# Last rows of a graph network kernel: 42 of 98 tiles added to the output by accumulating transfers instead of being loaded, added and stored

## The chip, the cores and the metric

The kernel runs on one core of one Trainium2 chip. The metric is the device time of one execution in microseconds. Three runs of the kernel before gave 2598.17 us as their median (2597.89 to 2601.66).

## The reference, cut to what matters

The layer normalizes x (12500 rows of 256), adds to x a graph convolution (`h @ W2.T + b2` over edges) and a hyperbolic attention block, and then applies a feed-forward block to the half of the rows with the largest routing weight:

```python
x = x + gnn(xn, ...) + mix(xn, ...)          # "x2"
x = x + ffn(layernorm(x))                    # all rows get layernorm(x) added, and
                                             # only the selected ones the product below
# in ffn, with xl = layernorm(x):
weights = xl @ wr + br                       # 12500 numbers
_, idx = top_k(weights, 6250); sel = idx[:6249]
h = gelu(xl[sel] @ w1 + b1); y = h @ w2 + b2
processed = zeros.at[sel].set(y * weights[sel][:, None])
return processed + xl
```

Which rows are selected is known only after all 12500 weights are. So the kernel writes `x2 + layernorm(x2)` for every row to the output first (the "base"), computes y for every row, and at the end adds `mask * y`, where `mask` is the weight of a selected row and 0 for another.

## The kernel before, in words

The rows are cut into 98 tiles of 128 (the last has 84 rows), and the tiles into 49 pairs (`NS`). After a first stage that normalizes x, a loop of 49 steps runs edges, attention, graph convolution and, for an earlier pair, the feed-forward block (`ffn_hidden`, `ffn_project`, `ffn_result`). SyncE stores the base of each pair to `out` (L712 to L715, counted by `base_stored`). The 42 pairs 0 to 41 get their y in the loop; the seven pairs of `LATE`, 42 to 48, get it behind the loop.

y isn't kept in a buffer of its own. `ffn_result(m)` (L947) adds the bias to the PSUM bank with y of pair m and writes it over `h0T` (the SBUF tensor `resident`), at `[:, t % 2, (t // 2) * 256 ...]` for tile t, and raises `y_read`. There is one bank for y, so TensorE starts `ffn_project(m, 0)` only when `y_read` has counted m results (L1268).

While TensorE works on the late pairs, VectorE searches the threshold of the top k in `route_vector`: eleven turns, each with a small matmul (L1333), then ranks and `mask_w` (L1460), one column for each tile. `ffn_result` of the pairs 42 to 45 stands among these turns. Behind them comes `last_vector`, and beside it `last_sync` on SyncE:

- The base is read back from `out` in 14 chunks of 7 tiles (896 KB). There are eight homes for them (`flat`, in buffers that have become free). The first eight are loaded as soon as all of the base is stored (L1496), long before the mask is there. Chunks 8 to 13 are loaded again into homes whose chunk has been stored (L1500 to L1503): SyncE waits for the store of chunk c - 2 and then issues the load of chunk c + 6.
- VectorE goes through the chunks in order: for each tile one `scalar_tensor_tensor`, base + mask * y (L1522), written into the home; `row_ready` tells SyncE, which stores the chunk (L1490 to L1492).
- `ffn_result` of the pairs 46, 47 and 48 stands ahead of chunks 3, 7 and 11.
- At its end SyncE waits until all chunks are stored.

GpSimd's queue ends with `route_pool` (constants and two selects for the search); it has nothing to do in this last part. DMAs issued by SyncE go through queue q1 (hardware_dynamic), those of GpSimd through q0 (software_dynamic). The order of the work is the order in which each engine's program is written; there is no planner.

Of the kernel before, what the change touches and what calls it, by code (L numbers as in the profile page):

```python
# [6 lines left out]
ALU = mybir.AluOpType  # L7
# [6 lines left out]
P = 128  # L14
D = 256
# [34 lines left out]
def build(nc, a, out):  # L50
    x, dst, edges = a["x"], a["dst"], a["edges"]
    N, E = x.shape[0], a["n_edges"]
    NT = -(-N // P)
    NS = NT // 2
    LAST = N - (NT - 1) * P
# [9 lines left out]
    with ExitStack() as ctx:  # L65
# [6 lines left out]
        def sem(name):  # L72
            return ctx.enter_context(nc.semaphore(name))
# [10 lines left out]
        h0T = resident[:, :].rearrange("p (c n) -> p c n", c=C)  # L84
# [30 lines left out]
        def view(base, at, *shape):  # L115
            n = 1
            for s in shape:
                n *= s
            v = base[:, at:at + n]
            if len(shape) == 2:  # L120
                v = v.rearrange("p (a b) -> p a b", b=shape[1])
            if len(shape) == 3:
                v = v.rearrange("p (a b c) -> p a b c", b=shape[1], c=shape[2])
            return v
# [41 lines left out]
        def tables_rows(pool):  # L166
            pool.dma_start(rows[:, :, :].bitcast(I32), dst.rearrange("(c p j) -> p c j", p=P, j=P)
                           ).then_inc(rows_landed, 16)

        def tables_load(pool):  # L170
            pool.wait_ge(ends_out, 2)
            for k in range(2):
                pool.dma_start(tile_ends_dram[k], endsT[:EC, k, :]).then_inc(ends_stored, 16)
            pool.wait_ge(ends_stored, 32)
            pool.dma_start(ends_bc[:NT], tile_ends_dram.rearrange("k c j -> k (c j)").partition_broadcast(NT)
                           ).then_inc(ends_landed, 16)
# [41 lines left out]
        def tables_pool(pool):  # L218
            g = nc.gpsimd
            g.iota(iota[:, :], [[1, P]], base=0, channel_multiplier=0,  # L220
                   allow_small_or_imprecise_dtypes=True).then_inc(consts_ready, 1)
            g.iota(iota_m, [[1, EC * P]], base=0, channel_multiplier=0,
                   allow_small_or_imprecise_dtypes=True).then_inc(consts_ready, 1)
            g.iota(thr, [[0, 1]], base=0, channel_multiplier=P,
                   allow_small_or_imprecise_dtypes=True).then_inc(consts_ready, 1)
            g.memset(zeros, 0.0).then_inc(consts_ready, 1)
            g.memset(ones, 1.0).then_inc(consts_ready, 1)
            pool.wait_ge(consts_ready, 5)
            g.affine_select(out=ident[:, :], in_=zeros, compare_op=ALU.not_equal, fill=1.0, base=0,
                            pattern=[[-1, P]], channel_multiplier=1).then_inc(consts_ready, 1)  # L230
            g.memset(mixW, 0.0).then_inc(consts_ready, 1)
# [426 lines left out]
        base_stored = sem("base_stored")  # L658
        x3_turned, x3T_ready, hid_done, hid_read = sem("x3_turned"), sem("x3T_ready"), sem("hid_done"), sem("hid_read")
        y_done, y_read = sem("y_done"), sem("y_read")  # L660
# [14 lines left out]
        LATE = list(range(m_next, NS))  # L675
# [268 lines left out]
        def y_rows(m):  # L944
            return h0T[:, :, 2 * m * P:2 * (m + 1) * P]

        def ffn_result(m):  # L947
            nc.vector.wait_ge(y_done, m + 1)
            nc.vector.tensor_tensor(y_rows(m), Y_BANK[:, :].rearrange("p (t d) -> p t d", d=D),
                                    fb2_row[:, :].unsqueeze(1).broadcast_to([P, 2, D]), ALU.add).then_inc(y_read, 1)  # L950
# [418 lines left out]
        ROUND_TRIES = [1, 1] + [TRIES] * ROUNDS  # L1369
        VISITS = 4  # L1370
        at = lambda n, w: work[:, n:n + w]
        wm, vv, flag, gt, eq, pre, incl, selm = (at(100 * q, NT) for q in range(8))
        mask_w = at(800, NT)
# [14 lines left out]
        def only_nodes(pool, dst_ap, src_ap):  # L1388

            return nc.gpsimd.affine_select(out=dst_ap, in_=src_ap, compare_op=ALU.is_ge, fill=LOWEST, base=N - 1,  # L1390
                                           pattern=[[-P, NT]], channel_multiplier=-1)

        def route_pool(pool):
            pool.wait_ge(slot_used, RING + NT * SLOTS)
            nc.gpsimd.memset(all_ones, 1.0).then_inc(route_consts, 1)
            pool.wait_ge(route_consts, 1)
            nc.gpsimd.affine_select(out=below, in_=all_ones, compare_op=ALU.is_gt, fill=0.0, base=0,
                                    pattern=[[1, P]], channel_multiplier=-1).then_inc(route_consts, 1)
            for b, value in enumerate(steps):
                ins = nc.gpsimd.memset(bits[:, b:b + 1], value)  # L1400
            ins.then_inc(route_consts, 1)
            pool.wait_ge(out_ready, 2 * NS)
            only_nodes(pool, wm, route_w[:, :]).then_inc(wm_ready, 1)
            pool.wait_ge(v_scaled, 1)
            only_nodes(pool, vv, vv).then_inc(vv_ready, 1)
# [57 lines left out]
        CH = 7  # L1463
        NCH = NT // CH
        flat = [view(rings, D * (2 + CH * n), CH, D) for n in range(3)]
        flat += [view(work, 2560 + CH * D * n, CH, D) for n in range(3)]
        flat += [view(weights, CH * D * n, CH, D) for n in range(2)]
        HOMES = len(flat)
        assert NT % CH == 0 and HOMES < NCH <= 2 * HOMES - 2
        row_landed = [sem(f"row_landed{c}") for c in range(NCH)]  # L1470
        row_stored = [sem(f"row_stored{c}") for c in range(NCH)]
        row_ready = sem("row_ready")

        def home(c):
            return flat[c % HOMES]

        def last_sync(sp):
            def parts(c):
                if c < NCH - 1:
                    return [(out[c * CH * P:(c + 1) * CH * P].rearrange("(t p) d -> p t d", p=P), home(c))]  # L1480
                first = c * CH * P
                return [(out[first:first + (CH - 1) * P].rearrange("(t p) d -> p t d", p=P), home(c)[:, 0:CH - 1]),
                        (out[first + (CH - 1) * P:N], home(c)[:LAST, CH - 1])]

            def load(c):
                for rows_, buf in parts(c):
                    sp.dma_start(buf, rows_).then_inc(row_landed[c], 16)

            def store(c):
                sp.wait_ge(row_ready, c + 1)  # L1490
                for rows_, buf in parts(c):
                    sp.dma_start(rows_, buf).then_inc(row_stored[c], 16)  # L1492

            sp.wait_ge(base_stored, 16 * NS + 16)
            sp.wait_ge(w2_done, NS)
            for c in range(HOMES):  # L1496
                load(c)
            for c in range(NCH):
                store(c)
                again = c - 2 + HOMES  # L1500
                if HOMES <= again < NCH:
                    sp.wait_ge(row_stored[c - 2], 16)
                    load(again)  # L1503
            for c in range(NCH):
                sp.wait_ge(row_stored[c], 32 if c == NCH - 1 else 16)

        def last_vector(dve):
            v = nc.vector
            seen = 1 + (len(ROUND_TRIES) + 1) // VISITS
            result_at = {}  # L1510
            for n, m in enumerate(LATE[seen:]):
                result_at[3 + 4 * n] = m
            assert LATE[0] * 2 >= (max(result_at) + 1) * CH
            for c in range(NCH):
                if c in result_at:
                    ffn_result(result_at[c])
                if c * CH + CH > LATE[0] * 2:
                    dve.wait_ge(y_read, NS)
                dve.wait_ge(row_landed[c], 32 if c == NCH - 1 else 16)
                for n in range(CH):  # L1520
                    t = c * CH + n
                    ins = v.scalar_tensor_tensor(home(c)[:, n], h0T[:, t % 2, (t // 2) * 2 * P:(t // 2 + 1) * 2 * P],  # L1522
                                                 mask_w[:, t:t + 1], home(c)[:, n], ALU.mult, ALU.add)
                ins.then_inc(row_ready, 1)

        @block.sync
        def _(sp):
            norm_sync(sp)
            main_sync(sp)
            last_sync(sp)  # L1530

        @block.gpsimd
        def _(pool):
            tables_rows(pool)
            tables_pool(pool)
            tables_load(pool)
            params_pool(pool)
            tables_bounds(pool)
            main_pool(pool)
            route_pool(pool)  # L1540

        @block.scalar
        def _(act):
# [4 lines left out]
        @block.vector  # L1548
        def _(dve):
            tables_vector(dve)  # L1550
            norm_vector(dve)
            main_vector(dve)
            route_vector(dve)
            last_vector(dve)
# [56 lines left out]
```

## Time and profile before

| | us |
|---|---|
| median of three runs (lowest, highest) | 2598.17 (2597.89, 2601.66) |
| the profiled execution, its own time | 2600.18 |
| its span (first to last instruction) | 2598.6 |
| mean granted TensorE clock | 0.982 of full speed |
| busy: TensorE matmul, VectorE, GpSimd, ScalarE | 2466.0, 1804.1, 1768.3, 1462.8 |
| DMA moved, mean over the span | 333.45 MB, 128 GB/s |

The table is read so: TensorE is busy 95% of the span, and all the rest of the kernel hides behind it. The profiled execution took 1.58 us more than its span, and 2.01 us more than the median of the runs. The change touches only the part from about 2542 us on, so the stretches of that part matter more than any mean.

### The profile page before, as it was taken

The numbers are of one execution on the slowest core, as the hardware profiler recorded it, in microseconds if no ns is written. First come the engines' busy times: TensorE is split into PE (matmuls) and PEld (weight loads), VectorE is DVE, ScalarE is ACT, GpSimd is POOL, SyncE is SP. The second block draws the span as 40 slices with busy tenths as digits, with TensorE's granted clock in tenths as the row PEclk, the third lists the DMA queues.
The fourth block names the chain that finished last, engine by engine and source line by source line (L and its number), as shares of the span: only waits on it lengthen the run. The fifth ranks groups of instructions, "written<-read, shape, count | busy, mean of one in ns | idle before, by whom it ended". The sixth has DMA issues, their size and how long they took to land.

```text
span 2598.6 us, 42298 instructions
## 1 busy us (share of the span) xinstructions
PE 2466.0 (95%) x12655; PEld 2168.7 (83%) x12655; DVE 1804.1 (69%) x5988; ACT 1462.8 (56%) x3513; POOL 1768.3 (68%) x1879
## 2 busy tenths in 40 slices
PE   4788999999999999999999999999999999999997
PEld 3677888888888888888888888888888888888886
DVE  6847676676776767767667676676866767767657
ACT  3756565565655656556555565565655656556431
POOL 2037777777777777777777777777777777777500
PEclk9898999999999999999999999999999999999998
DMA  7643434444344344444444434444444444343338
GB/s 231 193 133 101 128 113 121 124 117 129 116 121 125 114 121 123 121 126 115 119 124 117 130 113 121 123 116 126 117 120 124 116 125 117 114 129 114 97 117 282
DMA packets 192006, 333.45 MB, mean 128 GB/s; under 512 B 46286, under 2 KB 133964, under 8 KB 191672
## 3 DMA queue, kind: packets, MB, share of 16 engines
q0 software_dynamic: 86752, 238.17, 32.0%
q1 hardware_dynamic: 105018, 92.42, 11.1%
q8 instruction: 113, 1.85, 0.3%
q14 instruction: 123, 1.01, 0.1%
HBM read 291.99 MB, written 38.46 MB: 127 GB/s over the span
## 4 chain that ended last, share of the span: by engine, by line
PE 79%; DVE 10%; DMA 5%; ACT 5%; issue 1%; POOL 0%; SPq 0%; DVEq 0%; POOLq 0%
PE bank L1165 24%; PE qkv L1260 13%; PE bank L1272 12%; PE bank L1179 10%; PE bank L1209 6%; PE qkv L1189 4%; DMA work<-in_x 4%; PE qkv L1188 2%; PE bank L1225 2%; PE bank L1234 2%; DVE rings L968 2%; PE bank L1199 2%; DVE work L386 1%; DVE work L415 1%; ACT work L804 1%
## 5 line engine op out<-in xcount | busy, mean ns | idle before, releaser
L774 POOL DMA_INDIRECT rings<-xn_dram,window x1764 | 1742.4, 988 | 617.5 <-issue 382.3
L1165 PE MATMUL bank<-rings 128*128 128x256 f32 x3528 | 884.7, 380 | 17.4 <-DVE rings L968 14.2
L1165 PEld LDWEIGHTS bank<-rings 128*128 128x128 f32 x3528 | 656.9, 190 | 110.7 <-DVE rings L968 24.0
L968 DVE TENSOR_SCALAR rings<-iota,window_dst,window 128x128 f32<-128x128 f32 x1764 | 561.5, 363 | 142.2 <-PE bank L1165 127.9
L1260 PE MATMUL qkv<-work,ffn_weights 128*128 128x256 f32 x1568 | 364.4, 381 | 0.0
L1272 PE MATMUL bank<-ffn_weights,work 128*128 128x256 f32 x1568 | 361.9, 379 | 0.0
L864 ACT ACTIVATE work<-qkv,fb 128x256 f32<-128x256 f32 x392 | 160.1, 473 | 311.4 <-PE qkv L1260 310.9
L1272 PEld LDWEIGHTS bank<-ffn_weights,work 128*128 128x128 f32 x1568 | 297.2, 190 | 40.0
L1260 PEld LDWEIGHTS qkv<-work,ffn_weights 128*128 128x128 f32 x1568 | 295.0, 191 | 38.2
L1179 PE MATMUL bank<-resident,weights 128*128 128x256 f32 x1176 | 280.4, 382 | 0.0
L1179 PEld LDWEIGHTS bank<-resident,weights 128*128 128x128 f32 x1176 | 225.4, 192 | 31.1
L791 ACT ACTIVATE work<-qkv 128x1536 bf16<-128x1536 f32 x98 | 142.2, 1451 | 188.2 <-PE qkv L1189 188.2
L846 ACT ACTIVATE work<-bank 128x512 f32<-128x512 f32 x49 | 29.3, 598 | 315.5 <-PE bank L1217 315.5
L1189 PE MATMUL qkv<-weights,work 128*128 128x128 f32 x1176 | 205.0, 279 | 0.0
L1209 PE MATMUL bank<-weights,work 128*128 128x256 f32 x784 | 191.0, 387 | 0.1
L1188 PE MATMUL qkv<-ident,work 128*128 128x128 f32 x588 | 163.5, 278 | 23.5 <-ACT work L810 22.1
L1189 PEld LDWEIGHTS qkv<-weights,work 128*128 128x128 f32 x1176 | 182.2, 195 | 1.4
L877 ACT ACTIVATE work<-bank,cols 128x256 f32<-128x256 f32 x294 | 150.1, 566 | 57.6 <-PE bank L1179 57.6
L1026 DVE SCALAR_TENSOR_TENSOR work<-work,cols,bank 128x256 f32<-128x256 f32 x98 | 46.5, 475 | 189.3 <-PE bank L1165 189.3
L1209 PEld LDWEIGHTS bank<-weights,work 128*128 128x128 f32 x784 | 149.5, 193 | 27.1 <-ACT work L821 5.8
L1031 DVE TENSOR_TENSOR work<-work,b_row 128x512 f32<-128x512 f32 x49 | 34.1, 696 | 138.7 <-DMA work<-in_x 138.6
L1188 PEld LDWEIGHTS qkv<-ident,work 128*128 128x128 f32 x588 | 85.7, 146 | 34.5 <-issue 32.2
(243 smaller groups left out, 3346.2 us busy)
## 6 DMA issues: line engine op xcount, KB each, us to landing
rings<-xn_dram,window POOLq DMA_INDIRECT x1764, 2.8
xn_dram<-work SPq DMA_DIRECT2D x14, 896.0 KB, 7.7
work<-xn_dram SPq DMA_DIRECT2D x49, 256.0 KB
work<-in_x SPq DMA_DIRECT2D x48, 256.0 KB
out<-work SPq DMA_DIRECT2D x48, 256.0 KB
work<-in_x SPq DMA_DIRECT2D x9, 896.0 KB, 5.7
rings<-out SPq DMA_DIRECT2D x6, 896.0 KB, 8.8
out<-rings SPq DMA_DIRECT2D x6, 896.0 KB, 6.3
```

Source lines behind the costliest of these rows:

```text
L774: nc.gpsimd.indirect_dma_start(out=msg[q][:, :], out_offset=None, in_=xn_dram[:, :], in_offset=bass.IndirectOffsetOnAxis(ap=window[t % WIN ...
L791: s.activation(sq_dump, qkv.rearrange("p r i s c -> p (r i s c)"), ACT.Square, accum_out=nsq[h]).then_inc(nsq_ready, 1)
L864: ins = s.activation(hT[:, k], HID_BANK[q][:, e * D:(e + 1) * D], ACT.Gelu_apprx_tanh, bias=fb1[:, k:k + 1])
L877: ins = s.activation(h2T[:, k], H1_BANK[q][:, e * D:(e + 1) * D], ACT.Relu, scale=bn_a[:, k:k + 1], bias=bn_b[:, k:k + 1])
L968: v.tensor_scalar(sel[k % SEL_RING], iota[:, :], window_dst[b][:, k % SLOTS:k % SLOTS + 1], window[b][:, k % SLOTS, 2:3].bitcast(F32), ALU ...
L1165: te.matmul(agg[h][:, 0:D], sel[k % SEL_RING], msg[q], start=first, stop=last, skip_group_check=True).then_inc(slot_used, 1)
L1179: ins = te.matmul(H1_BANK[q][:, e * D:(e + 1) * D], wqkvT[:, c, k * P:(k + 1) * P], h0T[:, c, 2 * i * P:2 * (i + 1) * P], start=(c == 0), ...
L1188: te.transpose(qkv[:, k // 2, k % 2, 0, :], lhs, ident[:, :])
L1189: ins = te.matmul(qkv[:, k // 2, k % 2, 1, :], lhs, mixW[:, k, :], start=True, stop=True)
L1209: ins = te.matmul(FT_BANK[h][:, 0:D], outT[:, c], wresT[:, c], start=(c == 0), stop=(c == 3))
L1260: ins = te.matmul(HID_BANK[q][:, e * D:(e + 1) * D], fw1[:, c, k * P:(k + 1) * P], x3T[:, c], start=(c == 0), stop=(c == C - 1))
L1272: ins = te.matmul(Y_BANK[:, h * D:(h + 1) * D], hT[:, k, h * P:(h + 1) * P], fw2[:, k], start=(k == 0 and h == 0), stop=(k == HC - 1), ski ...
```

## The change

Only chunks 0 to 7 (tiles 0 to 55, pairs 0 to 27) are still loaded, added and stored by SyncE. For tiles 56 to 97 (pairs 28 to 48) VectorE multiplies y by the mask in place, and GpSimd issues transfers from `h0T` to `out` that add to what is in DRAM (`accum_op=ALU.add`). There are five such handovers, of 7, 7, 4, 2 and 1 pairs, with two transfers each (even tiles, odd tiles), so ten transfers. VectorE's order is written out in `ORDER` ("add" is a chunk as before, "scale" the new step for a range of pairs, "result" is `ffn_result`). `last_pool` is called at the end of GpSimd's program, behind `route_pool`.

```diff
-        row_landed = [sem(f"row_landed{c}") for c in range(NCH)]
-        row_stored = [sem(f"row_stored{c}") for c in range(NCH)]
-        row_ready = sem("row_ready")
+        ORDER = [("scale", 28, 35), ("add", 0), ("result", LATE[seen]), ("add", 1), ("scale", 35, 42), ("add", 2), ("add", 3),
+                 ("add", 4), ("result", LATE[seen + 1]), ("add", 5), ("scale", 42, 46), ("add", 6), ("add", 7), ("scale", 46, 48),
+                 ("result", LATE[seen + 2]), ("scale", 48, 49)]
+        SCALED = [o[1:] for o in ORDER if o[0] == "scale"]
+        row_landed = [sem(f"row_landed{c}") for c in range(HOMES)]
+        row_stored = sem("row_stored")
+        row_ready, y_scaled, row_added = sem("row_ready"), sem("y_scaled"), sem("row_added")
...
             for c in range(HOMES):
-                load(c)
-            for c in range(NCH):
-                store(c)
-                again = c - 2 + HOMES
-                if HOMES <= again < NCH:
-                    sp.wait_ge(row_stored[c - 2], 16)
-                    load(again)
-            for c in range(NCH):
-                sp.wait_ge(row_stored[c], 32 if c == NCH - 1 else 16)
+                sp.dma_start(home(c), rows_of(c)).then_inc(row_landed[c], 16)
+            for c in range(HOMES):
+                sp.wait_ge(row_ready, c + 1)
+                sp.dma_start(rows_of(c), home(c)).then_inc(row_stored, 16)
+            sp.wait_ge(row_stored, 16 * HOMES)
+            sp.wait_ge(row_added, 32 * len(SCALED))
+
+        def last_pool(pool):
+            pool.wait_ge(base_stored, 16 * NS + 16)
+            for u, (a_, b_) in enumerate(SCALED):
+                pool.wait_ge(y_scaled, u + 1)
+                for h in range(2):
+                    if b_ == NS and h == 1:
+                        pool.dma_start(out[(NT - 1) * P:N], h0T[:LAST, h, 2 * a_ * P:2 * b_ * P], accum_op=ALU.add
+                                       ).then_inc(row_added, 16)
+                    else:
+                        rows_ = out[2 * a_ * P:2 * a_ * P + (b_ - a_) * 2 * P - (P if b_ == NS else 0)]
...
+                            rows_ = rows_.rearrange("(m c p) d -> c p m d", c=2, p=P)[h]
+                            pool.dma_start(rows_, h0T[:, h, 2 * a_ * P:2 * b_ * P].rearrange("p (m d) -> p m d", d=D),
+                                           accum_op=ALU.add).then_inc(row_added, 16)
 
         def last_vector(dve):
...
+            for what, *which in ORDER:
+                if what == "result":
+                    ffn_result(which[0])
+                elif what == "add":
+                    c = which[0]
+                    dve.wait_ge(row_landed[c], 16)
+                    for n in range(CH):
+                        t = c * CH + n
+                        ins = v.scalar_tensor_tensor(home(c)[:, n], y_of(t), mask_w[:, t:t + 1], home(c)[:, n],
+                                                     ALU.mult, ALU.add)
+                    ins.then_inc(row_ready, 1)
+                else:
+                    a_, b_ = which
+                    dve.wait_ge(y_read, b_)
+                    for t in range(2 * a_, 2 * b_):
+                        ins = v.tensor_scalar(y_of(t), y_of(t), mask_w[:, t:t + 1], None, ALU.mult)
+                    ins.then_inc(y_scaled, 1)
...
             route_pool(pool)
+            last_pool(pool)
```

## Rows read from the trace of the kernel before

**Rows 1.** The page: busy time of each engine.

```profile
PE 2466.0 (95%) x12655; PEld 2168.7 (83%) x12655; DVE 1804.1 (69%) x5988; ACT 1462.8 (56%) x3513; POOL 1768.3 (68%) x1879
```

**Rows 2.** Stretches of the last part: busy us (instructions) by engine, clock, DMA share, GB/s.

```profile
2494.30:2516.00 21.70, 21.70 (x110) 19.02 (x110) 14.97 (x42) 6.30 (x16) 0.27 (x1) 1.00 1.01 322
2545.60:2557.00 11.40, 11.40 (x56) 10.06 (x55) 11.39 (x29) 3.60 (x9) 0.00 (x0) 1.00 0.90 272
2557.00:2575.00 18.00, 18.00 (x87) 15.86 (x86) 15.52 (x39) 4.82 (x12) 0.00 (x0) 1.00 1.08 382
2575.00:2596.00 21.00, 4.14 (x20) 3.30 (x18) 11.14 (x28) 0.00 (x0) 0.00 (x0) 0.66 1.09 385
2596.00:2598.60 2.60, 0.00 (x0) 0.00 (x0) 0.00 (x0) 0.00 (x0) 0.00 (x0) 0.50 0.23 80
```

**Rows 3.** The chain of waits from 2570 us on: start us, us, what.

```profile
2573.96 5.20 PE bank L1272 x24
2579.15 0.02 issue
2579.18 0.17 DVE resident L949
...
2585.01 3.17 DVE work L1522 x8
```

**Rows 4.** Timeline of VectorE behind the mask: start us, us, instruction, idle before.

```profile
2542.40 0.26 DVE L1460 TENSOR_TENSOR work<-work,route_w 128x98 f32<-128x98 f32 x1
2542.70 8.40 DVE L1522 SCALAR_TENSOR_TENSOR rings<-resident,work,rings 128x256 f32<-128x256 f32 x21
2551.11 0.69 DVE L949 TENSOR_TENSOR resident<-bank,fb_row 128x512 f32<-128x512 f32 x1
...
2565.36 0.69 DVE L949 TENSOR_TENSOR resident<-bank,fb_row 128x512 f32<-128x512 f32 x1 [2.48 <-PE bank L1272]
...
2579.18 0.69 DVE L949 TENSOR_TENSOR resident<-bank,fb_row 128x512 f32<-128x512 f32 x1 [2.04 <-PE bank L1272]
```

**Rows 5.** Timeline of SyncE's DMA issues in the last part: start us, us, transfers.

```profile
2545.59 5.91 SPq L1492 DMA_DIRECT2D out<-rings  x3
...
2583.61 9.72 SPq L1492 DMA_DIRECT2D out<-work  x4
```

**Rows 6.** DMA packets from 2542 us to the end: queue, packets, MB, share of 16 engines.

```profile
q1 hardware_dynamic: 18180, 18.26, 93.1%
```

**Rows 7.** Durations (ns, min/median/max) by line, first and last start us.

```profile
L267 DVE TENSOR_SCALAR resident<-resident,rings x1: 1087/1087/1087, 56.2 to 56.2; 98x1664 f32<-98x1664 f32 x1
L1452 DVE TENSOR_SCALAR work<-work x1: 273/273/273, 2537.7 to 2537.7; 128x98 f32<-128x98 f32 x1
L1522 DVE SCALAR_TENSOR_TENSOR rings<-resident,work,rings x42: 475/478/485, 2542.7 to 2576.7; 128x256 f32<-128x256 f32 x42
```

**Rows 8.** A run of seven two-column tensor_scalar in the first stage, timeline.

```profile
91.81 2.35 DVE L415 TENSOR_SCALAR work<-rings,work 128x256 f32<-128x256 f32 x7
```

**Rows 9.** Timeline of TensorE, project of pair 48 (L1272).

```profile
2570.34 1.89 PE L1272 MATMUL bank<-ffn_weights,work 128*128 128x256 f32 x8
```

**Rows 10.** GpSimd's direct DMA issues: ns min/median/max; then time to landing us.

```profile
L167 POOL DMA_DIRECT2D resident<-in_dst x1: 1357/1357/1357, 1.5 to 1.5; - x1
L193 POOL DMA_DIRECT2D weights<-in_w_pw x4: 572/573/619, 21.7 to 23.5; - x4
tile_ends_dram<-rings POOLq DMA_DIRECT2D x2, 6.5 KB, 1.7
rings<-xn_dram,window POOLq DMA_INDIRECT x1764, 2.8
```

**Rows 11.** DMA queues of the whole span: packets, MB, share of 16 engines.

```profile
q0 software_dynamic: 86752, 238.17, 32.0%
```

**Rows 12.** GpSimd's issues and VectorE's tensor_scalar side by side in the loop, durations.

```profile
L774 POOL DMA_INDIRECT rings<-xn_dram,window x1764: 942/946/1465, 163.8 to 2450.0; - x196
L968 DVE TENSOR_SCALAR rings<-iota,window_dst,window x1764: 327/343/574, 165.9 to 2456.8; 128x128 f32<-128x128 f32 x196
```

More of the change, by code:

```diff
@@ L1468, in build, with rows_of @@
         HOMES = len(flat)
-        assert NT % CH == 0 and HOMES < NCH <= 2 * HOMES - 2
-        row_landed = [sem(f"row_landed{c}") for c in range(NCH)]
-        row_stored = [sem(f"row_stored{c}") for c in range(NCH)]
-        row_ready = sem("row_ready")
+        LOADED = HOMES * CH
+        assert LOADED % 2 == 0 and LOADED < 2 * LATE[0]
+        seen = 1 + (len(ROUND_TRIES) + 1) // VISITS
+        ORDER = [("scale", 28, 35), ("add", 0), ("result", LATE[seen]), ("add", 1), ("scale", 35, 42), ("add", 2), ("add", 3),
+                 ("add", 4), ("result", LATE[seen + 1]), ("add", 5), ("scale", 42, 46), ("add", 6), ("add", 7), ("scale", 46, 48),
+                 ("result", LATE[seen + 2]), ("scale", 48, 49)]
+        SCALED = [o[1:] for o in ORDER if o[0] == "scale"]
+        assert LATE[seen + 2] == NS - 1 and SCALED[0][0] * 2 == LOADED and SCALED[-1][1] == NS
+        row_landed = [sem(f"row_landed{c}") for c in range(HOMES)]
+        row_stored = sem("row_stored")
+        row_ready, y_scaled, row_added = sem("row_ready"), sem("y_scaled"), sem("row_added")
         def home(c):
-            return flat[c % HOMES]
+            return flat[c]
+        def rows_of(c):
+            return out[c * CH * P:(c + 1) * CH * P].rearrange("(t p) d -> p t d", p=P)
         def last_sync(sp):
[L1478 to L1492, printed above, removed]
             sp.wait_ge(base_stored, 16 * NS + 16)
@@ new lines, in last_sync @@
+            sp.wait_ge(row_stored, 16 * HOMES)
[10 more added lines that the diff above has]
+                        rows_ = out[2 * a_ * P:2 * a_ * P + (b_ - a_) * 2 * P - (P if b_ == NS else 0)]
+                        if b_ == NS:
+                            pool.dma_start(rows_, h0T[:, h, 2 * a_ * P:2 * b_ * P], accum_op=ALU.add).then_inc(row_added, 16)
+                        else:
+                            rows_ = rows_.rearrange("(m c p) d -> c p m d", c=2, p=P)[h]
+                            pool.dma_start(rows_, h0T[:, h, 2 * a_ * P:2 * b_ * P].rearrange("p (m d) -> p m d", d=D),
+                                           accum_op=ALU.add).then_inc(row_added, 16)
@@ L1507, in last_vector @@
         def last_vector(dve):
             v = nc.vector
[L1509 to L1524, printed above, removed]
+            y_of = lambda t: h0T[:, t % 2, (t // 2) * 2 * P:(t // 2 + 1) * 2 * P]
@@ new lines, in last_vector @@
+            for what, *which in ORDER:
[9 more added lines that the diff above has]
+                    ins.then_inc(row_ready, 1)
+                else:
+                    a_, b_ = which
[3 more added lines that the diff above has]
+                    ins.then_inc(y_scaled, 1)
```

## The prediction
> **What bounds the kernel now.** I read the page first: TensorE is busy 95% of the span [rows 1], so over most of it nothing else counts. The change begins behind the mask, so I then read the last part by stretches. The reader is to see there where TensorE stops: it is full until 2575, has 4.14 us left in the next stretch, and nothing behind that, while the DMA engines run at a share of 1.08 to 1.09 and 382 to 385 GB/s from 2557 to 2596 [rows 2]. The chain of waits gives the place: TensorE ends at 2579.15, and the chain goes over to VectorE, whose last addition ends at 2588.18 (2585.01 + 3.17) [rows 3]. The chain stops at that last instruction; the span goes on to 2598.6. What lies between is SyncE's stores, whose last issues go from 2583.61 to 2593.33 although VectorE has long handed everything over [rows 5]. So the last part is bound by the transfers: 18.26 MB by q1 [rows 6]. That is 12.80 MB of stores (12500 rows of 1 KB) and 5.46 MB of loads of chunks 8 to 13 (5332 rows). At 385 GB/s these take 47.4 us; they have 2545.6 to 2596.6. The end of full flow, 2596.6, I get from the last stretch: 80 GB/s over 2.6 us is 0.21 MB or 0.54 us at full rate [rows 2]. Behind it stand 2.0 us of last packets and the final wait. The missing 3.6 us are the start (the first store) and the thinner stretch up to 2557, at 272 GB/s [rows 2].
>
> Two floors lie below: TensorE with 2579.15, and VectorE behind it.
>
> **VectorE, step by step.** An addition costs 8.40/21 = 0.400 us in a run, 0.396 behind the first (its duration is 0.478, it overlaps the next by 0.082) [rows 4, 7]. 42 go. 42 `tensor_scalar` with one column come. The trace has none of 256 columns; with one column operand, 98 columns take 273 ns and 1664 take 1087 [rows 7], 0.52 ns for each more, so 256 take 0.355 us. Less the same overlap that is 0.273 in a run. The bound from above is the two-column form at 2.35/7 = 0.336 [rows 8], beyond that 0.396. I take 0.273: VectorE has 42 x (0.396 - 0.273) = 5.2 us less.
>
> The schedule from 2542.70 [rows 4]:
> - scale 28-35 (14 tiles, 3.8 us) to 2546.5; add 0 to 2549.3; result 46 waits for TensorE until 2551.11, as y isn't there before (1.8 us idle, behind it add 1 and the second handover wait); free at 2551.7.
> - add 1 to 2554.5, scale 35-42 to 2558.3, add 2 to 4 to 2566.6. Result 47 is read at once (y is there since 2565.36) and counted at 2567.3. TensorE needs it at 2570.34 [rows 9]: 3.1 us of cover. If a multiplication cost 0.396, 28 of them would take 3.4 us more, and TensorE would be held by 0.4.
> - add 5 to 2570.0, scale 42-46 to 2572.2, add 6 and 7 to 2577.8, scale 46-48 to 2578.9; result 48 waits for TensorE to 2579.18, as before; scale 48 ends at 2580.4.
>
> So VectorE ends at 2580.4 instead of 2588.2, 7.8 us earlier. That is worth something only if the transfers end with it.
>
> **SyncE.** Six chunks of loads and six of stores go, with their waits. It stores eight chunks, each ready earlier than the transfers get to it, except chunk 0 (2549.4 in place of 2545.6).
>
> **GpSimd.** It has one instruction of 0.27 us in the stretch from 2494.3 and none behind it [rows 2], so its ten issues delay nothing of its own. An issue costs 0.57 us for small ones and 1.36 for the one with 1664 runs [rows 10]; one with 896 rows I put at 1.0, bounds 0.6 to 1.4. Ten are under 10 us beside 34. Of the first one the wakeup and about 1.4 us until data flow are on the path: first data at 2546.5 + 0.1 + 1.4 = 2548.0. Of the last ones nothing is, if the queue is still full then. If it is not, two issues of 0.6 and a landing of 2.8 [rows 10] end the kernel: 2580.4 + 0.1 + 1.2 + 2.8, some 2584.5 to 2585.5.
>
> **The transfers, which decide.** Plain stores: 7168 rows, 7.34 MB, 19.1 us at 385 GB/s. Accumulated rows: 5.46 MB, 14.2 us multiplied by f, where f is the price of an accumulated row in plain ones. The trace shows no accumulating transfer, so f is bounded. Below: it costs no more than the store that it replaces, f = 1, 14.2 us. Above: an accumulated row is fetched from DRAM and from SBUF and written once, thus what the load and the store of before moved, and it does that at the rate of q0's packets: 238.17 MB in 32.0% of 2598.6 us (831.6 us) are 286 GB/s [rows 11], so f = 2 x 385/286 = 2.7, 38.3 us. Nearest is f = 2: two fetches at the rate of the saturated stretch, in which loads and stores are mixed and together reach 385 [rows 2]. I take f = 2, 28.4 us. Sum: 2548.0 + 19.1 + 28.4 = 2595.5, plus 2.0 behind the flow: 2597.5. On the way the queues never run dry: handover 1 and chunk 0 keep them until 2559.9, chunk 1 until 2562.3, and handover 2 is issued at 2558.4.
>
> So 18.26 MB of packets become 7.34 stored and twice 5.46: the same 47.4 us. What was saved is the thinner stretch at the start (3.6 us before, against 2548.0 - 2545.6 = 2.4 now): 1.1 us. The profiled execution would be 2600.18 - 1.1 = 2599.1, and the median of the runs 2598.17 - 1.1 = **2597.1**.
>
> From the trace, a load and a store together flow as fast as stores alone, so the fetches seem to share one limit in each DMA engine. The Trainium skill says the same of an added reduction (Collectives: The Full Stack, "The bandwidth ceiling"): the addition itself is free, the two source reads on one ring halve the rate, 62.28 against 32.35 GB/s. By that ratio f would be 1.93, an estimate, and the end 1.0 us earlier. No row here shows it. The same section has 32.35 GB/s on two DMA engines; as an estimate 16 would add at 259 GB/s, so f = 1.49, which is the first rival at its f of 1.5.
>
> **Rivals.**
> 1. Accumulating is cheaper than load and store (f 1.0 to 1.7): the second fetch is partly hidden behind the first. For it: the copies are of 1 KB runs, and a copy may be limited at its SBUF end rather than in the engine. Against it: mixed loads and stores use both directions and still stop at 385. With f = 1.5: 2588.4 + 2.0 = 2590.4, median 2590.0. With f = 1 the queues run dry (the stores and handovers are waited for), and the last issues set 2585.5, median 2585.1.
> 2. The other side: an accumulated row flows no faster than q0's packets. Place: the 5332 rows on q0; price at 286 GB/s of fetches: 38.3 us in place of 28.4, end 2607.4, median 2607.0. It decides against the change from f = 2.43 on (158 GB/s of accumulated rows), where the end is 5.2 us behind that of before. For it: q0's share in the loop. Against it: those packets are small batches of 128 scattered rows, in which an engine waits more than it moves.
> 3. GpSimd's issues are late. In the loop GpSimd's issue takes up to 1.465 us against 0.946, and the tensor_scalar up to 0.574 against 0.343 [rows 12]: they do get in each other's way, half a us at a time. The Trainium skill has this as a lock (SBUF — State Buffer, "SBUF: two separate sides"): GpSimd can't write descriptors during a two-port operation of VectorE; the trace agrees in sign. Here handover 1 meets only additions, and ten issues by 0.5 us are 5 us on an idle engine; on the path are 1.0 us at most. It costs more only where the queue's room for rows runs out and GpSimd waits in the middle of a handover: then q0 stops between handovers, and I put 3 to 8 us on it, median 2601 to 2605.
> 4. TensorE waits for result 47 (the dear multiplication): 0.4 us, and only visible under rival 1.
>
> **How the numbers follow.** A change of under 0.2% (5.2 us) can't be told from none. The forecast (f from 1.70 to 2.43, ends 2593.3 to 2603.6) gets 0.40, all of it no change. Rival 1 gets 0.34, all faster. Rival 2 gets 0.20 and rival 3 0.06, slower in all. The forecast's own range is 2593 to 2603; the other cases reach to 2585 and 2607, beyond that where a row is dearer still. The range 2587 to 2609 leaves out the cheapest tenth and the dearest.
>
> **What would show it.** The packets of q0 in the last part: their share times the stretch, over 5.46 MB, gives f at once. DMA share near 1.09 from 2548 to about 2595 says the forecast; a share falling before 2585 says rival 1; q0 still alone at 2600 says rival 2. VectorE's last instruction should end at 2580.4, each multiplication taking 0.355, and TensorE should still end at 2579.2. Wrong would make it: any f outside 1.7 to 2.43, or a hole in the flow between 2548 and 2590.

## The result, and the profile after

The changed kernel takes 2602.61 us (median of 22 runs), the kernel before 2598.59 beside it: ratio 1.0013, 95% interval 1.0007 to 1.0019. So it is slower by 0.13%: 3.4 us by the ratio, 4.0 by the two medians. That is less than the 0.2% that the prediction called no change, but beyond the interval. The prediction had the time in its range and the sign of its small difference wrong: 1.1 us faster.

The page of the changed kernel, its span and engines [rows 1]:

```profile
span 2599.9 us, 42287 instructions
PE 2461.7 (95%) x12655; PEld 2167.7 (83%) x12655; DVE 1800.4 (69%) x5988; ACT 1460.8 (56%) x3513; POOL 1780.4 (68%) x1889
```

The span of one execution says little, as the loop ahead of the mask varies by some us. So I compare the last part, from the first instruction that uses the mask to the end of the span. It starts at 2542.70 before [rows 4] and at 2540.42 here (timeline of VectorE, columns as in [rows 4]):

```profile
2540.12 0.26 DVE L1460 TENSOR_TENSOR work<-work,route_w 128x98 f32<-128x98 f32 x1
2540.42 3.77 DVE L1533 TENSOR_SCALAR resident<-resident,work 128x256 f32<-128x256 f32 x14
2544.10 2.86 DVE L1526 SCALAR_TENSOR_TENSOR rings<-resident,work,rings 128x256 f32<-128x256 f32 x7
2548.83 0.69 DVE L949 TENSOR_TENSOR resident<-bank,fb_row 128x512 f32<-128x512 f32 x1 [1.87 <-PE bank L1272]
...
2564.19 0.69 DVE L949 TENSOR_TENSOR resident<-bank,fb_row 128x512 f32<-128x512 f32 x1
...
2577.62 0.83 DVE L1533 TENSOR_SCALAR resident<-resident,work 128x256 f32<-128x256 f32 x2
```

The last part is 2598.6 - 2542.7 = 55.9 us before and 2599.9 - 2540.4 = 59.5 us after: 3.6 us more, which agrees with the timed runs. Times below that are "behind the mask" count from there.

The stretches that answer to [rows 2], two shorter ones around the first data, and the queues between 2562 and 2590:

```profile
2545.60:2557.00 11.40, 11.40 (x54) 10.06 (x53) 9.53 (x29) 2.51 (x6) 3.46 (x3) 1.00 1.00 186
2557.00:2575.00 18.00, 18.00 (x87) 15.85 (x87) 18.00 (x49) 4.68 (x11) 5.11 (x4) 1.00 1.17 244
2575.00:2596.00 21.00, 1.85 (x9) 1.30 (x7) 2.86 (x8) 0.00 (x0) 4.24 (x4) 0.59 1.16 260
2546.50:2547.00 0.50, 0.50 (x4) 0.45 (x3) 0.46 (x2) 0.00 (x0) 0.50 (x2) 1.00 0.00 0
2547.00:2547.50 0.50, 0.50 (x4) 0.45 (x3) 0.00 (x0) 0.00 (x0) 0.50 (x1) 1.00 0.48 39
2547.25:2550.00 2.75, 2.75 (x15) 2.42 (x14) 1.17 (x3) 0.00 (x0) 1.07 (x1) 1.00 1.15 155
```

```profile
q0 software_dynamic: 3290, 3.29, 72.6%
q1 hardware_dynamic: 3408, 3.42, 44.5%
```

The reader is to see three things. From 2557 on the DMA engines are full, as they were before: share 1.16 to 1.17, against 1.08 to 1.09 (a share above 1 says that packets of one engine overlap in time). An accumulated row is counted once (5.46 MB for 42 tiles in all), so 240 GB/s here are 117 accumulated and 122 stored. The two queues send about as many packets of 1 KB there, 3290 and 3408. And the first data come at 2547.25, 6.8 us behind the mask, where the stores of before began 3.8 us behind it. GpSimd's part of that:

```profile
2544.81 3.51 POOL L1512 DMA_DIRECT2D out<-resident  x2 [51.96 <-DVE resident L1533]
...
2556.26 3.27 POOL L1512 DMA_DIRECT2D out<-resident  x2 [7.94 <-DVE resident L1533]
...
L1533 DVE TENSOR_SCALAR resident<-resident,work x42: 334/349/571, 2540.4 to 2578.1; 128x256 f32<-128x256 f32 x42
```

A handover has two issues, and the second starts before the first has ended. The two of 896 rows take 3.51 us together in handover 1 and 3.27 in handover 2, so 1.75 and 1.64 for each; the very first takes 1.82 by itself.

### The profile page after: what moved, and what is told of

The parts are those of the page before. It is cut to its first block, busy times and chain, and to the rows that moved or that the text cites. A ratio compares the mean times of both kernels' runs of the same rounds, so it can differ in the third digit from the quotient of the medians.

```text
span 2599.9 us, 42287 instructions
## 1 busy us (share of the span) xinstructions
PE 2461.7 (95%) x12655; PEld 2167.7 (83%) x12655; DVE 1800.4 (69%) x5988; ACT 1460.8 (56%) x3513; POOL 1780.4 (68%) x1889
## 3 DMA queue, kind: packets, MB, share of 16 engines
q14 instruction: 123, 1.01, 0.1%
## 4 chain that ended last, share of the span: by engine, by line
PE 79%; DVE 10%; ACT 4%; DMA 4%; issue 1%; SPq 0%; POOL 0%; POOLq 0%; DVEq 0%
PE bank L1165 25%; PE qkv L1260 13%; PE bank L1272 12%; PE bank L1179 10%; PE bank L1209 6%; PE qkv L1189 4%; DMA work<-in_x 3%; PE qkv L1188 2%; PE bank L1225 2%; PE bank L1234 2%; PE bank L1199 2%; DVE rings L968 2%; DVE work L386 1%; DVE work L415 1%; PE bank L1246 1%
## 5 line engine op out<-in xcount | busy, mean ns | idle before, releaser
L1272 PE MATMUL bank<-ffn_weights,work 128*128 128x256 f32 x1568 | 362.0, 379 | 0.0
L1272 PEld LDWEIGHTS bank<-ffn_weights,work 128*128 128x128 f32 x1568 | 297.6, 190 | 39.7
```

Of the source, the lines that this page charges most:

```text
L1272: ins = te.matmul(Y_BANK[:, h * D:(h + 1) * D], hT[:, k, h * P:(h + 1) * P], fw2[:, k], start=(k == 0 and h == 0), stop=(k == HC - 1), ski ...
```

## The experiments

Every run's last part, read as above, and its timed ratio to the kernel before where there is one. The first four experiments (e1 to e4) ran on a chip that took 2992 us for the kernel before, with a granted clock of 0.93 in place of 0.98; VectorE's schedule behind the mask was the same there to 0.1 us, so these four are read by their last part.

| run | last part, us | ratio to before (interval) |
|---|---|---|
| kernel before; again | 55.9; 55.8 | |
| changed kernel | 59.5 | 1.0013 (1.0007, 1.0019) |
| e1_plain | 47.9 | 0.9975 (0.9949, 1.0000) |
| e2_alone | 46.0 | 0.9974 (0.9947, 1.0000) |
| e3_long_runs | 55.0 | 0.9996 (0.9967, 1.0025) |
| e4_chunk_first | 59.8 | 1.0004 (0.9975, 1.0034) |
| e5_last_merged | 59.8 | 1.0017 (1.0008, 1.0026) |
| e6_stores_first | 61.2 | 1.0020 (1.0010, 1.0029) |
| e7_14_tiles | 55.9 | 1.0006 (0.9996, 1.0015) |
| e8_long_alone | 45.8 | |
| e9_stores_queued | 51.1 | |
| e11_small_first; again (e13) | 57.4; 57.0 | 0.9995 (0.9963, 1.0026); 1.0011 (1.0002, 1.0020) |
| v1_reload_by_gpsimd | 55.6 | 1.0001 (0.9992, 1.0010) |
| v2_first_in_pieces | 55.3 | 0.9996 (0.9987, 1.0005) |
| v3_ninth_home | 53.0 | 0.9995 (0.9986, 1.0004) |
| v4_five_more_tiles | 52.0 | 0.9985 (0.9958, 1.0013) |
| v5_whole_first | 52.4 | 0.9990 (0.9981, 0.9999) |

**b0_before_again.**

> The kernel before, unchanged, for a second reading of the last part from the first addition behind the mask to the end: 55.9 us in the first profile. Theory: this stretch does not depend on what the chip or the throttle does to the loop before it, so 55.9 within 0.3. Rival: it varies by some us from execution to execution; then differences under 2 us between the profiles say nothing.

55.8: the last part repeats to 0.1 us here, and to 0.4 in the one relative of the changed kernel that has two profiles (e11 and e13). The changed kernel itself has one.

**What the addition costs: e1_plain, e2_alone, e9_stores_queued.**

```diff
-  pool.dma_start(rows_, ..., accum_op=ALU.add)
+  pool.dma_start(rows_, ...)
```

> The changed kernel with its ten transfers as plain writes: the addition to DRAM is left out, so tiles 56 to 97 get only mask * y. VectorE, GpSimd's issues and SyncE are as in the changed kernel. Theory A (the transfers' own flow is the cost: an accumulated row costs 2.2 plain ones): 12.8 MB at 385 GB/s are 33 us, less than the 37 us that VectorE takes from the mask to its last handover, so the end is set by the last issues and landing: some 42 to 44 us behind the mask (59.5 in the changed kernel), time about 0.6% below the changed one. Theory B (the late start and GpSimd's issues, 1.2 to 2.4 us each, are the cost and the flow is not): the end comes at least 55 us behind the mask, time within 0.2% of the changed one. GpSimd's issue of 896 rows: 1.75 us if the addition does not make it dearer, 1.2 or less if it does.

The end moved from 59.5 to 47.9 us: theory A. It missed my 42 to 44, since the writes flowed at 322 GB/s and not at 385. GpSimd's two issues of 896 rows fell from 3.51 to 2.00 us together, from 1.75 to 1.00 for each, and the first data came 6.0 us behind the mask in place of 6.8. One more thing changed than the addition: q0's plain writes are packets of 4 KB in the trace (1326 of them), the accumulating ones of 1 KB (5332). An issue of 896 rows has 896 packets when it accumulates and 224 when it doesn't, and that may be what shortens it (see the price of a run). What larger packets alone do to the flow of plain writes wasn't tried; SyncE's plain stores are of 1 KB and flow at 341 GB/s alone (below).

```profile
2945.50:2985.00 39.50, 30.12 (x142) 26.18 (x140) 29.23 (x81) 7.20 (x17) 6.02 (x9) 0.91 0.98 322
2943.57 2.00 POOL L1512 DMA_DIRECT2D out<-resident  x2 [51.94 <-DVE resident L1532]
```

```diff
-  for c in range(HOMES):
-      sp.wait_ge(row_ready, c + 1)
-      sp.dma_start(rows_of(c), home(c)).then_inc(row_stored, 16)
+  sp.wait_ge(row_ready, HOMES)
```

> The changed kernel with SyncE's eight stores left out (tiles 0 to 55 stay without mask * y). The accumulating transfers have the DMA engines for themselves. Theory A1 (an accumulated row costs two fetches and some more, whatever is beside it): 385/2.2 = 175 GB/s while handovers 1 and 2 flow. Theory A2 (alone each row waits for its own fetch, and only a second queue fills these gaps): about 140 GB/s as in the first 3 us of the changed kernel's flow, and then 3.67 MB of handovers 1 and 2 take 26 us. Rival B: no slower than stores, 300 GB/s or more, with idle engines between handovers. End: set by the last handovers under all, 43 to 46 us behind the mask, about 0.5% below the changed kernel.

Both A1 and A2 missed, on the dear side. A stretch of e2_alone in which q0 has work throughout:

```profile
2947.40:2951.40 4.00, 4.00 (x20) 3.53 (x19) 4.00 (x14) 2.10 (x6) 0.00 (x0) 1.00 1.23 193
```

By steps of 2 us the full stretches read 188 to 200 GB/s, typically 195. Against 385 that is f = 1.97. (In e6_stores_first q0 is alone for 18 us, at 198 GB/s: 1.94.) Against the 341 GB/s of plain stores that are alone too (e9_stores_queued, next) it is 1.75. The Trainium skill's ratio for a reduction against a copy (Collectives: The Full Stack, "The bandwidth ceiling"), 1.93, agrees with the first; the like comparison, each alone, gives less.

```diff
+  v.memset(at(1900, 1), 0.0).then_inc(mask_made, 1)       # at the mask
-      sp.wait_ge(row_ready, c + 1)
+      sp.wait_ge(row_landed[c], 16)                        # behind one wait for mask_made
-  last_pool(pool)
```

> The changed kernel reduced to its eight plain stores: they are all issued as soon as the mask is there, without VectorE's additions (left out, as are the accumulating transfers). TensorE works beside them as before. It gives the rate of queued stores alone. Reading 1: 385 GB/s, as for the last stores of the kernel before; then a mixed flow of 240 GB/s (117 accumulated, 122 stored) means 5.8 us for each accumulated MB against 5.1 alone, a price of mixing of 0.7 us per MB, and the 331 to 347 GB/s of stores early in the last part are VectorE's rate of supply. Reading 2: 350 GB/s or less; then mixing costs 0.4 or less, and the stores that lose their loads lose rate.

Reading 2, as far as it goes. Queued stores alone in e9_stores_queued, and the last stores of the kernel before:

```profile
2542.00:2560.00 18.00, 11.29 (x55) 9.59 (x53) 1.50 (x6) 3.84 (x9) 0.00 (x0) 0.94 1.04 341
```

```profile
2590.00:2596.00 6.00, 0.00 (x0) 0.00 (x0) 0.00 (x0) 0.00 (x0) 0.00 (x0) 0.50 1.09 386
```

341 GB/s here, also while TensorE stood still (344 from 2554 to 2560, where the row has no matmul); yet stores behind a mixed flow run at 385. Why stores alone have two rates is not settled.

**The price of a run: e3_long_runs, e8_long_alone.**

```diff
-  rows_ = rows_.rearrange("(m c p) d -> c p m d", c=2, p=P)[h]
-  pool.dma_start(rows_, h0T[...].rearrange("p (m d) -> p m d", d=D), accum_op=ALU.add)
+  rows_ = rows_.rearrange("(c p m) d -> c p (m d)", c=2, p=P)[h]
+  pool.dma_start(rows_, h0T[...], accum_op=ALU.add)
```

> The changed kernel, but the rows of a handover are laid so that each partition adds to neighbouring rows in DRAM: one run of 7 KB (4 KB, 2 KB) in place of 7 (4, 2) of 1 KB. It adds y to the wrong rows; bytes, order and waits are the same. Theory A1 (the price is bytes: two fetches for one write): f stays at 2.0 to 2.2, time within 0.2% of the changed kernel, at best 3 us less. Theory A2 (the price is a fixed one for each run of a row): f falls to 2.0 or below, flow of both queues together from 240 to over 270 GB/s, the end 4 to 8 us earlier. GpSimd's issue: down from 1.75 us to about 0.8 if it goes by the number of runs.

> Both changes at once: runs of 7, 4 and 2 KB in DRAM (the rows added to are not the right ones) and SyncE's eight stores left out. With 1 KB runs and the engines for themselves the accumulating transfers flow at 197 GB/s. Theory bytes (two fetches for each write are all of the price): 190 to 210 GB/s here too, and the 4.5 us that long runs brought beside the stores are the mixing, which gets cheaper with long runs. Theory run (a fixed price for each run): 220 GB/s or more alone.

With long runs the end came 4.5 us earlier. Of that 0.8 is the earlier start: two issues took 1.91 us in place of 3.51 (e3_long_runs), and data came 6.0 us behind the mask. So a long issue isn't owed to the addition alone: with 128 packets an accumulating issue takes 0.96 us, with 896 it takes 1.75, and the plain one of e1_plain with 224 takes 1.00. No run has both forms with the same number of packets, so what the addition itself adds to an issue stays open. With the engines to itself (e8_long_alone) the flow was 219 GB/s (208 to 222 by 2 us):

```profile
2931.90 1.91 POOL L1512 DMA_DIRECT2D out<-resident  x2 [51.94 <-DVE resident L1533]
```

```profile
2553.20:2557.20 4.00, 4.00 (x20) 3.54 (x19) 3.63 (x9) 1.02 (x3) 0.00 (x0) 1.00 1.07 219
```

So part of the price goes by the run, as A2 had it, but most of it by bytes. With the best 2 us of each, 200 and 222 GB/s on 16 engines, a run of 1 KB takes 82 ns and one of 7 KB 517: that is 10 ns for the run and 72 for each KB, which two fetches of 36 would make. A plain 1 KB row at 385 takes 42.6 ns. The two forms differ in the rows' places in DRAM too, which I didn't separate.

**Order and start: e4_chunk_first, e6_stores_first, e11_small_first.**

```diff
-  ORDER = [("scale", 28, 35), ("add", 0), ("result", ...
+  ORDER = [("add", 0), ("scale", 28, 35), ("result", ...
```

> The changed kernel with chunk 0 ahead of the first handover on VectorE, nothing else. In the changed kernel data flow from 6.9 us behind the mask on, in the kernel before from 3.9. Theory start (the flow is continuous to the end, so each us of an earlier start is one gained): stores from 3.9 us on, while GpSimd issues the first handover at 7.2 and not at 4.4; 2.4 us of work done before, end 2 to 2.5 us earlier, time 0.1% below the changed kernel, that is level with before. Rival (the last handovers set the end): no change.

59.8: no gain. Chunk 0 flowed early, and then the engines stood idle until the later handover's data came (e4_chunk_first):

```profile
2927.00:2929.50 2.50, 2.50 (x13) 2.21 (x12) 2.36 (x9) 0.00 (x0) 0.00 (x0) 1.00 0.94 315
2929.50:2932.00 2.50, 2.50 (x13) 2.19 (x12) 0.77 (x2) 0.00 (x0) 2.01 (x2) 1.00 0.02 7
```

This run also shows that VectorE isn't what makes an issue long. The first one starts here while VectorE is idle (2929.4 to 2931.2), and it takes 1.82 us (the two 3.51), as in the changed kernel beside VectorE's additions:

```profile
2929.99 3.51 POOL L1512 DMA_DIRECT2D out<-resident  x2 [54.73 <-DVE resident L1533]
```

```diff
-  ORDER = [("scale", 28, 35), ("add", 0), ("result", LATE[seen]), ("add", 1), ...
+  ORDER = [("add", 0), ("add", 1), ("add", 2), ("result", LATE[seen]), ("add", 3), ("add", 4), ("add", 5), ("scale", 28, 35),
+           ("add", 6), ("result", LATE[seen + 1]), ("add", 7), ("scale", 35, 42), ("scale", 42, 46), ("scale", 46, 48),
```

> The changed kernel with VectorE's order turned: the chunks that SyncE stores come first (the first handover stands behind chunk 5, the second behind chunk 7), so that stores and accumulating transfers overlap little. Bytes and transfers are the same. Flow seen so far: accumulating alone 197 GB/s (5.1 us per MB), mixed with stores 240 GB/s together, from which an accumulated MB costs 5.5 to 5.8 us. Theory mixing (the two queues hinder each other, 0.5 us or so for each accumulated MB): end 56.5 to 57.5 us behind the first instruction after the mask, against 59.5. Rival (an accumulated row costs the same beside stores; order does not matter): 59 to 60. Rival gap (the first handover is later, and the engines are idle before it): over 60.

61.2: the gap won, and the profile shows it. Stores alone flow no faster than VectorE finishes chunks (0.917 MB in 2.77 us, 331 GB/s), the engines are idle for 2 us and more before the handover's data, and q0 alone is left at the end (e6_stores_first):

```profile
2564.00:2566.00 2.00, 2.00 (x11) 1.77 (x10) 2.00 (x6) 0.00 (x0) 2.00 (x2) 1.00 0.01 1
2582.00:2600.00 18.00, 0.00 (x0) 0.00 (x0) 0.00 (x0) 0.00 (x0) 3.55 (x4) 0.50 1.23 198
```

So the order is worth some us, but this run can't price the mixing.

```diff
-  ORDER = [("scale", 28, 35), ("add", 0), ...
+  ORDER = [("scale", 28, 29), ("scale", 29, 35), ("add", 0), ...
```

> The changed kernel with its first handover cut in two, pair 28 alone and then pairs 29 to 34. The first data should flow from about 3.6 us behind the mask and not from 6.9. Unlike chunk 0 first, this leaves no hole, as GpSimd goes on issuing. Theory start (the late first data are part of the loss and are kept to the end): end 1.5 to 3 us earlier, 56.5 to 58 us against 59.5 behind the mask. Rival (supply in the first ten us bounds the flow, as with the first chunk in pieces, where an earlier start brought 0.3): under 0.5 us.

> The changed kernel with pair 28 handed over alone ahead of pairs 29 to 34, timed in more rounds than the first time, where the interval was too wide (0.9963 to 1.0026) for a difference of 2 us. From the profile (57.4 us behind the mask against 59.5 in the changed kernel and 55.8 before): time 0.06% above the kernel before, against 0.13% for the changed kernel. If the late first handover were not part of the loss, 0.13% again.

57.4 and 57.0: 2.1 to 2.5 us of the 3.6 come back, so the late start is the larger part of the loss. The data start 3.9 us earlier, but not all of that is kept, as they flow thinly at first. The timed rounds (1.0002 to 1.0020) are consistent with that and don't prove it. First data in e11_small_first flow 3 us behind the mask (2552.83):

```profile
2555.00:2556.00 1.00, 1.00 (x8) 0.90 (x7) 1.00 (x5) 0.38 (x2) 1.00 (x2) 1.00 0.31 22
2557.00:2560.00 3.00, 3.00 (x16) 2.64 (x15) 2.50 (x7) 0.00 (x0) 2.92 (x2) 1.00 0.66 69
```

**How many tiles, and the last handover: e7_14_tiles, e5_last_merged.**

```diff
 (in the kernel before)
-  for c in range(NCH): store(c) ...
+  for c in range(NCH - 2): store(c) ...
+  if c == 3: scale(42, 46)      # behind result 46
+  if c == 8: scale(46, 48)
+  scale(48, 49)                 # behind the last chunk; six accumulating transfers
```

> The kernel before with only its last two chunks (tiles 84 to 97, pairs 42 to 48) accumulated by GpSimd, in handovers of 4, 2 and 1 pairs; chunks 8 to 11 are reloaded and stored by SyncE as before. Theory rate (each accumulated tile costs 0.2 to 0.3 plain ones more than load and store): a third of the 42 tiles, a third of the 3.6 us: 57.1 us behind the mask. Theory start (the 3.6 us come mainly from the first handover, which delays the first store and begins slowly): here chunk 0 is first as before, so 55.9 or less. Rival: 59 or more, if the last handovers are what ends late.

55.9, as before, with 14 tiles accumulated and chunk 0 first: accumulating a tile costs what loading and storing it does, as far as 14 tiles can show it beside a scatter of 0.4 us, when the start isn't delayed. Theory start.

```diff
-  ("scale", 46, 48), ("result", LATE[seen + 2]), ("scale", 48, 49)]
+  ("result", LATE[seen + 2]), ("scale", 46, 49)]
```

> The changed kernel with its last two handovers (pairs 46-47 and pair 48) made one, behind the last result: the step of handing the last pairs over singly is undone. When they are handed over, the queues hold some 15 us of older transfers, so theory backlog says: no change of the end, 59.5 us behind the mask within 0.3. Rival: the end hangs on the last handover, then 1 to 2 us later.

59.8, within 0.3: the separate handover of the last pairs was worth nothing here, as the queues still held older transfers.

**Fewer bytes in the kernel before: v1 to v5.**

```diff
-  again = c - 2 + HOMES; sp.wait_ge(row_stored[c - 2], 16); load(again)       # SyncE
+  for c in range(HOMES, NCH): pool.wait_ge(row_stored[c - HOMES], 16); load   # GpSimd
```

> The kernel before; the six reloads (chunks 8 to 13) are issued by GpSimd as plain loads, each as soon as the store of the chunk that held the home has landed, in place of by SyncE between two stores. Same bytes. Before, the flow is thin (200 GB/s) from 11 to 14 us behind the mask, as SyncE issues a reload only behind the next store but one. Theory thin stretch: up to 1.5 us come back, end 54.5 to 55.3 us behind the mask against 55.9. Rival (loads on the second queue crowd out the stores, so that homes come free later and VectorE waits for chunks): 56 to 58.

```diff
+  chunk 0: stores of tiles 0-1, 2-3, 4-6, each when VectorE has finished it
```

> As v1, and the first chunk is stored in three pieces (2, 2 and 3 tiles) as VectorE finishes them, so that data flow from 2 us behind the mask and not from 3.9. Theory (the flow is continuous from there, so an earlier start is kept): 1.5 us less than v1, end 53 to 54 us behind the mask, time 0.1% below before. Rival (as with chunk 0 first in the changed kernel, the gain is lost again in a hole behind it): level with v1.

```diff
+  spare = [(0, 3, view(weights, 2 * CH * D, 3, D)), (3, 5, view(work, 2048, 2, D)), (5, 7, view(work, 7936, 2, D))]
+  HOMES = len(flat) + 1
```

> As v2, with a ninth home in columns that are free by then (3 tiles in weights, 4 in work): nine chunks are loaded before the mask is there, and five reloaded. 0.92 MB less behind the mask, 2.4 us at 385 GB/s. Theory (the last part is bound by bytes): end 2.0 to 2.5 us before v2's, 51 to 52 us behind the mask, time 0.15 to 0.2% below before. Rival: VectorE or the waits for chunks take over as the bound, then under 1 us.

```diff
+  more = [(0, 1, rings[:, 23 * D:24 * D]), (1, 2, b2_row[:, :]), (2, 3, bres_row[:, :]), (3, 4, wr_row[:, :]),
+          (4, 5, rem_msg[:, :])]     # tiles 0-4 of chunk 9, loaded ahead of the mask
```

> The kernel before with nine homes, reloads by GpSimd and the first chunk in pieces (as the run with a ninth home), and with five more single tiles loaded ahead into columns that are free by then, so that 30 tiles are reloaded behind the mask in place of 42 before. 1.57 MB less than before, 4.1 us at 385 GB/s. Theory bytes: end 1.7 us before the run with nine homes, 51.2 to 51.6 us behind the mask, time 0.15 to 0.2% below the kernel before and 0.3% below the changed one. Rival: VectorE (its additions alone end 45.5 us behind the mask, and the last stores follow) has become the bound: 52.5 or more.

> As the run with five more tiles loaded ahead, but with the first chunk stored whole again. The pieces brought 0.3 us beside the reloads by GpSimd alone. Theory (the first ten us are bound by VectorE's supply of finished chunks, 331 GB/s, not by when the first store starts): end 51.8 to 52.3 us behind the mask, as with the pieces (52.0), 3.7 us less than the kernel before, time 0.14% below it. Rival (a shorter flow makes the start count again): 53 or more.

Thin stretch (v1) and pieces (v2) brought 0.3 us each, within the scatter: both theories missed. v1 lies between its theory and its rival, v2 at its rival. The ninth home brought 2.3 us for 0.92 MB, as its bytes ask for (2.4). The five tiles brought 1.0 in place of 1.7, as the flow was at 355 to 360 GB/s towards the end there. v5, without the pieces, has 52.4 us and the ratio 0.9990 (0.9981 to 0.9999): it beats the kernel before by 0.1%, just clear of noise; its last part is 3.5 us shorter, which is as much. It wasn't timed beside the changed kernel; by their ratios to before it is 0.2% faster. Its flow (v5_whole_first):

```profile
2555.00:2567.00 12.00, 12.00 (x59) 10.60 (x58) 9.52 (x24) 2.93 (x7) 0.93 (x1) 1.00 1.04 356
2567.00:2593.00 26.00, 12.51 (x58) 10.68 (x57) 19.50 (x49) 3.35 (x8) 2.34 (x3) 0.80 1.06 373
```

## Why the prediction was wrong

**The bound: right.** The last part is bound by transfers. Taking the addition away moved the end by 11.6 us (e1_plain), and taking 0.92 MB of reloads away by 2.3 (v3_ninth_home).

**VectorE: right.** 14 multiplications took 3.77 us (3.8 predicted), one 0.349 (0.355), and it ended 38.0 us behind the mask (37.7). Result 47 was counted at 24.5 (24.6), and TensorE didn't wait.

**GpSimd's issue and the first data: wrong.** I put 1.0 us on an issue of 896 rows, bounds 0.6 to 1.4, from rows of plain loads [rows 10]; it took 1.75, the first one 1.82, outside the bounds. Those rows are of plain loads with other packets; with a quarter of the packets (e1_plain) or a seventh (e3_long_runs) an issue does take 1.0. Between VectorE's last multiplication and the first data I put 1.5 us; it took 0.62 to the issue and 2.44 from there to the data, which come 0.6 us behind the end of the first issue, here as in e1_plain and e3_long_runs. So the flow began 6.8 us behind the mask and not 5.3. Against the kernel before (3.8) that is 3.0 us later, of the 3.6 lost.

**The price f = 2: right for the transfers by themselves** (1.97 alone). **Wrong was that the sum flows at 385 throughout**, with nothing put down for a thin start or for two queues side by side. The flow lasted 50.6 us (59.5 - 6.8 and less 2.0 and the rounding) in place of 47.5. 0.5 us of it are the first 2.75 us at 155 GB/s; 2.0 are the 28 us from 2562 to 2590, in which 3.29 MB at 5.19 us and 3.42 MB at 2.60 us should have taken 26.0; the rest lies between. How much of the 2.0 is mixing is open: with the 341 GB/s of e9_stores_queued for the stores it is about 1 us, with 385 all of it. In the kernel before, the thin stretch that I counted as saved makes its flow 50.0 us long, so in flow alone the two kernels are level to 0.6 us, as e7_14_tiles shows from the other side.

In sum, 54.8 us predicted behind the mask, 59.5 measured: 1.5 from the start, 3.1 from the flow. The forecast gain was only 1.1 us, so either miss by itself turns its sign, and the flow is the larger one. The price of 2 was a choice between bounds of 1 and 2.7, as no row of before held an accumulating transfer; the runs bear it out. That the time lay in the range says little, as the range was 22 us wide.

**Rivals.** 1 (cheaper accumulating) and 2 (as dear as q0's packets) fell: f is 1.97, and 2.2 if all of the longer flow is put on the accumulated rows. 3 had the right place, GpSimd's issue, and the wrong reason: the first issue has nothing queued ahead of it and is as long beside an idle VectorE (e4_chunk_first), so it is long by itself. What it said of VectorE and GpSimd together holds at one place: a multiplication beside the last issues took 0.571 us, against 0.349 in the median. In e5_last_merged, where none meets an issue, the longest takes 0.354; but so it does in e3_long_runs, where the last ones meet a shorter issue. The Trainium skill's page on SBUF (SBUF — State Buffer, "SBUF: two separate sides") has the two engines share a pair of ports that one holds for a whole instruction while the other waits; the 0.571 agrees in sign, e3_long_runs shows no such wait. 4 didn't occur.

## What to carry to other kernels

An accumulating transfer replaces a load, an addition and a store on the compute engine's side, but not on the DMA engines': here it flows at about half the rate of a plain one, as a load and a store in its place would (that it fetches twice isn't seen in the trace, which counts its bytes once). Where the DMA engines are the bound nothing is saved. There only fewer bytes in the bound stretch help, such as loading ahead into whatever buffers are free by then. And where a flow is continuous to the end, the us until its first data are paid in full: hand over a small piece first, and check that nothing runs dry behind it (the earlier starts of e4_chunk_first and of the pieces in v2 were lost again).

## What the runs showed of the hardware that was not expected

- An accumulating transfer of 896 rows of 1 KB costs GpSimd 1.75 us to issue (mean of two), the same rows written plainly 1.00, accumulated in 128 runs of 7 KB 0.96. The trace has 896, 224 and 128 packets for them: plain writes of these rows leave GpSimd's queue as packets of 4 KB, accumulating ones as packets of 1 KB.
- The first data come 0.6 us behind the end of the first issue, whether that takes 1.82, 1.04 or 1.01 us (the changed kernel, e1_plain, e3_long_runs). In the changed kernel the first 2.75 us flow at 155 GB/s, where the steady state is 195.
- Queued plain stores flow at 341 GB/s by themselves and at 385 behind a mixed flow, at the same rows of 1 KB. No run explains it.
